# The edge stage of a graph kernel: 64-row products, a gathered layout with q left of x1, and copies moved between engines

## The reference

```python
h = silu(edge_scalars @ (Wfc1 / sqrt(16)));  w = h @ (Wfc2 / sqrt(64))
w0, w1, w2, w3 = w[:, :64], w[:, 64:128], w[:, 128:160], w[:, 160:192]
f0 = x0 @ Wl1_0 * a * inv8
f1 = einsum('num,uv->nvm', x1, Wl1_1) * a[..., None] * inv32
e0, e1 = f0[edge_src], f1[edge_src]
mid0 = w0 * e0 * sh0
mid1 = w3 * einsum('eum,em->eu', e1, sh1) / sqrt(3.0)
mid2 = w1[:, :, None] * e0[:, :, None] * sh1[:, None, :]
mid3 = w2[:, :, None] * e1 * sh0[:, :, None]
...
alpha = scal @ Wa * a * inv96;  out_s = scal @ Wl2_s * a * inv96
out_v = einsum('num,uv->nvm', vec, Wl2_v) * a[..., None] * inv96
x = layernorm(x + sc + alpha * concat([out_s, out_v]))
```

## Time and profile before

| what | value |
|---|---|
| time, median of 3 runs | 1123.99 us (1123.52 to 1131.0) |
| the profiled execution | 1131.23 us |
| its span, first to last instruction | 1129.4 us |
| mean granted clock of TensorE, of full speed | 0.981 |
| PE busy | 1029.3 us (91%) |
| PEld busy | 970.3 us (86%) |
| DVE busy | 975.0 us (86%) |
| ACT busy | 657.6 us (58%) |
| POOL busy | 752.1 us (67%) |

### The profile page before, as it was taken

The page is one execution under the profiler, slowest core; times in us unless marked ns, Lnnn a source line. Parts: engine busy times, 40 slices in busy tenths (PEclk is TensorE's granted clock), DMA queues, the critical chain, the costliest instruction groups (busy, mean ns, idle before and its releaser), DMA issues.

```text
span 1129.4 us, 33849 instructions
## 1 busy us (share of the span) xinstructions
PE 1029.3 (91%) x9020; PEld 970.3 (86%) x9020; DVE 975.0 (86%) x3758; ACT 657.6 (58%) x1865; POOL 752.1 (67%) x906
## 2 busy tenths in 40 slices
PE   4879999999999999999999869889988998898983
PEld 3869999999999999999999858777877887788883
DVE  3858888888888888888888849999999999999996
ACT  1324444444444444444444328888888888888877
POOL 6646666666666666666666247777777778778783
PEclk8989999999999999999999989999999999999997
DMA  5743343334334343434333268999999999999993
GB/s 161 156 134 109 103 112 103 109 103 112 109 105 110 98 115 103 112 102 110 106 108 111 68 167 217 253 242 246 257 254 241 247 254 252 244 251 249 261 249 106
DMA packets 170169, 184.95 MB, mean 164 GB/s; under 512 B 17831, under 2 KB 150247, under 8 KB 170152
## 3 DMA queue, kind: packets, MB, share of 16 engines
q1 hardware_dynamic: 151208, 152.15, 48.5%
q0 software_dynamic: 18944, 32.60, 13.9%
HBM read 119.73 MB, written 64.95 MB: 164 GB/s over the span
## 4 chain that ended last, share of the span: by engine, by line
PE 63%; DVE 13%; issue 9%; SPq 5%; POOL 3%; DMA 3%; ACT 3%; DVEq 0%; POOLq 0%; ACTq 0%
PE ps L646 15%; PE ps L659 10%; PE ps L636 7%; PE ps L710 5%; PE ps L654 4%; PE ps L634 4%; PE ps L625 4%; PE ps L619 4%; PE ps L656 3%; SPq L463 3%; DVE pre L1032 3%; PE ps L723 2%; DVE ra L1048 2%; PE ps L616 2%; DVE shift L1091 2%
## 5 line engine op out<-in xcount | busy, mean ns | idle before, releaser
L541 POOL DMA_INDIRECT gat<-table,src_now x392 | 374.1, 954 | 219.0 <-issue 115.7
L764 ACT ACTIVATE z<-ps 128x130 f32<-128x130 f32 x196 | 55.2, 282 | 291.7 <-PE ps L659 286.2
L578 POOL TENSOR_TENSOR xa<-xin 128x256 f32<-128x256 f32 x196 | 161.7, 846 | 94.9 <-DMA xin<-table 80.9
L646 PEld LDWEIGHTS ps<-h_sb,wt 128*128 128x128 f32 x1568 | 207.5, 193 | 11.6 <-issue 1.1
L646 PE MATMUL ps<-h_sb,wt 128*128 128x128 f32 x1568 | 208.0, 276 | 0.7 <-DVE mid L877 0.7
L805 ACT ACTIVATE fin<-res,shift,rstd 128x160 f32<-128x160 f32 x392 | 172.1, 511 | 53.8 <-DVE shift L1091 53.3
L710 PE MATMUL ps<-win,hot 64*128 64x162 f32 x2352 | 190.5, 308 | 4.0 <-ACT agg L796 3.9
L710 PEld LDWEIGHTS ps<-win,hot 64*128 64x128 f32 x2352 | 166.7, 187 | 22.6 <-issue 17.4
L597 POOL TENSOR_TENSOR res<-agg,pre 128x640 f32<-128x640 f32 x98 | 151.4, 1545 | 27.6 <-ACT agg L796 26.1
L659 PE MATMUL ps<-wy,mid 128*128 128x161 f32 x784 | 151.5, 316 | 0.0
L900 DVE SCALAR_TENSOR_TENSOR msg<-ps,sha,z 128x161 f32<-128x161 f32 x392 | 132.8, 381 | 4.9 <-ACT z L764 0.3
(11 more groups left out here) (102 smaller groups left out, 2046.2 us busy)
## 6 DMA issues: line engine op xcount, KB each, us to landing
win<-rows SPq DMA_DIRECT2D x392, 122.2 KB, 3.5
rows<-msg SPq DMA_DIRECT2D x98, 326.0 KB
xin<-table SPq DMA_DIRECT2D x98, 322.0 KB, 4.1
out<-fin SPq DMA_DIRECT2D x49, 640.0 KB, 5.3
gat<-table,src_now POOLq DMA_INDIRECT x392, 2.6
eas<-ea_t SPq DMA_DIRECT2D x5, 512.0 KB
wt<-weights SPq DMA_DIRECT2D x1, 929.5 KB, 4.7
shs<-sh_t SPq DMA_DIRECT2D x1, 752.0 KB
```

The source lines that it names most:

```text
L541: pool.indirect_dma_start(out=gat[:, n, 0:XW], out_offset=None, in_=table, in_offset=bass.IndirectOffsetOnAxis(ap=src_now[:, n:n + 1], axis=0)
L578: last = nc.gpsimd.tensor_tensor(xa[:, b0], xin[:, b, :, n:n + w], xin[:, b, :, 0:1].broadcast_to([P, GROUP, w]), ALU.mult)
L646: last = nc.tensor.matmul(w_ps[:, c, :], wt[:, w:w + P], h_sb[:, b1, :], start=True, stop=True)
```

## The change

All of it is in the edge stage, apart from the place of columns that the node stage reads.

- **w** is made by four products of 64 rows, one per tile and half of the columns, that use rows 0 to 63 and 64 to 127 of the array in turn and write into two banks, in place of four products of 128 rows. **e0** is made by two products of 64 rows in place of one of 128, and stands behind e1 now. The product for e1 is the same.
- **y** has two products of 97 columns and two of 161, before one of 130, one of 64 and two of 161.
- The nodes' rows are in three tables now, `table`, `turned` (x1, a, x0) and `spread` (x0, a, 32 zeros, x1). A pair's first tile is gathered from turned (161 columns), the second from spread (193), so that the x0 of both tiles lie side by side and PE can transpose them where they are: DVE's copy to `x0` goes. q lies left of x1 in both tiles.
- **mid** is one DVE instruction of 512 columns, before two of 256. ACT's copy of e is two instructions of 256 columns, before one of 384.
- The **label column** of msg is copied by ACT, before by DVE; DVE's msg waits for it by `label_ready`. DVE's **z** waits for ACT's copy (`zc_ready`), before for y itself.
- Before the loop, the row of heads goes to banks of w, PE waits there for `mid_ready`, DVE copies heads and the sum of wrong out of PSUM, and the fourth step's w waits for that.

```diff
-        e_ps = ps[:, 2, 0:3 * P].rearrange("p (c e) -> p c e", e=P)
-        w_ps = ps[:, 3, :].rearrange("p (c e) -> p c e", e=P)
-        y_ps = ps[:, 4, 0:2 * YW].rearrange("p (s w) -> p s w", s=2)
-        yb_ps = ps[:, 5, 0:2 * MUL1].rearrange("p (s w) -> p s w", s=2)
-        heads_ps = ps[:, 6, 0:T]
-        wrong_ps = ps[0:1, 7, 0:1]
+        e0_ps = ps[:, 2:4, 0:P]
+        e1_ps = ps[:, 2, P:3 * P]
+        w_ps = ps[:, 4:6, 0:2 * P]
+        y_ps = ps[:, 6:8, 0:YW]
+        heads_ps = ps[:, 4:6, 2 * P:2 * P + T // 2]
+        wrong_ps = ps[0:1, 4, 2 * P + T // 2:2 * P + T // 2 + 1]
...
                 pool.sem_inc(gather_go, 1)
-                for n in (2 * j, 2 * j + 1):
+                for s, of, first in ((0, turned, G_TURNED), (1, spread, G_SPREAD)):
+                    n = 2 * j + s
                     pool.indirect_dma_start(
-                        out=gat[:, n, 0:XW], out_offset=None, in_=table,
+                        out=gat[:, j, first:first + of.shape[1]], out_offset=None, in_=of,
...
-                    nc.tensor.transpose(t_ps[:, 0, :],
-                                        x0[:, b0].rearrange("p s w -> p (s w)"), ident[:])
+                    nc.tensor.transpose(t_ps[:, 0, :], gat[:, j, G_X0:G_X0 + P], ident[:])
                     for s in range(2):
                         last = nc.tensor.transpose(t_ps[:, 1 + s, :],
-                                                   gat[:, 2 * j + s, 1 + MUL0:GW], ident[:])
+                                                   gat[:, j, G_Q[s]:G_Q[s] + P], ident[:])
...
-                    nc.tensor.matmul(e_ps[:, 0, :], wt[:, W_E0:W_E0 + P], t_sb[:, b1, 0, :],
+                    nc.tensor.matmul(e1_ps, wt[:, W_E1:W_E1 + P],
+                                     t_sb[:, b1, 1:3, :].rearrange("p s e -> p (s e)"),
                                      start=True, stop=True)
-                    nc.tensor.matmul(e_ps[:, 1:3, :].rearrange("p s e -> p (s e)"),
-                                     wt[:, W_E1:W_E1 + P],
-                                     t_sb[:, b1, 1:3, :].rearrange("p s e -> p (s e)"),
-                                     start=True, stop=True).then_inc(e_ready, 1)
+                    for s in range(2):
+                        half = slice(s * MUL0, (s + 1) * MUL0)
+                        last = nc.tensor.matmul(e0_ps[:, s, :], wt[half, W_E0:W_E0 + P],
+                                                t_sb[half, b1, 0, :], start=True, stop=True)
+                    last.then_inc(e_ready, 1)
 
                     pe.wait_ge(h_out, done(i, j, 1))
                     if has(i, j, 2):
                         pe.wait_ge(mid_ready, done(i, j, 2))
-                    for c in range(4):
+                    if isinstance(i, int) and (i, j) == (0, 3):
+                        pe.wait_ge(heads_out, 2)
+                    for c in range(2):
                         w = W_W + c * P
-                        last = nc.tensor.matmul(w_ps[:, c, :], wt[:, w:w + P], h_sb[:, b1, :],
-                                                start=True, stop=True)
+                        for s in range(2):
+                            half = slice(s * FC_H, (s + 1) * FC_H)
+                            last = nc.tensor.matmul(w_ps[:, s, c * P:(c + 1) * P],
+                                                    wt[half, w:w + P], h_sb[half, b1, :],
+                                                    start=True, stop=True)
                     last.then_inc(w_ready, 1)
                 if alive(i, j, 2):
 
                     pe.wait_ge(mid_ready, done(i, j, 2))
                     if has(i, j, 3):
                         pe.wait_ge(msg_ready, done(i, j, 3))
-                    nc.tensor.matmul(y_ps[:, :, 0:1 + MUL0], mid[:, b2, 0, :],
-                                     wy[:, 0:W_YB - W_Y0], start=True, stop=True)
-                    nc.tensor.matmul(yb_ps.rearrange("p s w -> p (s w)"), mid[:, b2, 1, :],
-                                     wy[:, W_YB - W_Y0:W_Y1 - W_Y0], start=True, stop=True)
                     for s in range(2):
-                        last = nc.tensor.matmul(y_ps[:, s, 1 + MUL0:YW], mid[:, b2, 2 + s, :],
-                                                wy[:, W_Y1 - W_Y0:W_S0 - W_Y0],
+                        nc.tensor.matmul(y_ps[:, s, 0:W_Y1 - W_YA], mid[:, b2, s, 0:P],
+                                         wy[:, 0:W_Y1 - W_YA], start=True, stop=True)
+                        last = nc.tensor.matmul(y_ps[:, s, W_Y1 - W_YA:YW],
+                                                mid[:, b2, s, P:2 * P],
+                                                wy[:, W_Y1 - W_YA:W_S0 - W_YA],
                                                 start=True, stop=True)
                     last.then_inc(y_ready, 1)
...
+                pe.wait_ge(mid_ready, 2)
+                for n in range(2):
+                    last = nc.tensor.matmul(heads_ps[:, n, :], ones[0:1, :],
+                                            heads[:, n * (T // 2):(n + 1) * (T // 2)],
+                                            start=True, stop=True)
+                last.then_inc(heads_spread, 1)
...
-                    nc.scalar.activation(e_sb[:, b1].rearrange("p c e -> p (c e)"),
-                                         e_ps.rearrange("p c e -> p (c e)"),
-                                         ACT.Copy).then_inc(e_out, 1)
+                    nc.scalar.activation(e_sb[:, b1, :, P:2 * P],
+                                         e1_ps.rearrange("p (s e) -> p s e", s=2), ACT.Copy)
+                    nc.scalar.activation(e_sb[:, b1, :, 0:P], e0_ps, ACT.Copy).then_inc(e_out, 1)
+                if alive(i, j, 3):
+                    i3 = i if j == 3 else i - 1
+                    j3 = (j - 3) % PAIRS
+
+                    if has(i, j, 3 + PAIRS):
+                        act.wait_ge(messages_out[j3 // 2], 16 * (i3 + 0))
+                    else:
+                        act.wait_ge(dsts_ready, 1)
+                    nc.scalar.activation(msg[:, 2 * j3:2 * j3 + 2, LABEL],
+                                         dsts[:, bass.ds(i3 * BLOCK + 2 * j3, 2)],
+                                         ACT.Copy).then_inc(label_ready, 1)
                 if alive(i, j, 2):
...
-                    if has(i, j, 2):
-                        dve.wait_ge(t_ready, done(i, j, 2))
-                    nc.vector.tensor_copy(x0[:, b0], gat[:, n:n + 2, 1:1 + MUL0])
                     dve.wait_ge(qprod_ready, done(i, j))
-                    nc.vector.tensor_reduce(gat[:, n:n + 2, QX:GW], qprod[:], AX_X,
+                    nc.vector.tensor_reduce(of_pair(j, G_Q, MUL1), qprod[:], AX_X,
                                             ALU.add).then_inc(q_ready, 1)
...
-                    nc.vector.tensor_tensor(mid[:, b0, 0:2, :], w_ps[:, 0:2, :],
-                                            e_sb[:, b0, 0:1, :].broadcast_to([P, 2, P]),
-                                            ALU.mult)
-                    nc.vector.tensor_tensor(mid[:, b0, 2:4, :], w_ps[:, 2:4, :],
-                                            e_sb[:, b0, 1:3, :], ALU.mult
+                    nc.vector.tensor_tensor(mid[:, b0], w_ps, e_sb[:, b0], ALU.mult
                                             ).then_inc(mid_ready, 1)
                 if alive(i, j, 3):
 
-                    dve.wait_ge(y_ready, done(i, j, 3))
+                    dve.wait_ge(zc_ready, done(i, j, 3))
                     if has(i, j, 5):
                         dve.wait_ge(msg_ready, done(i, j, 5))
                     nc.vector.tensor_tensor(
                         z[:, b1, :, 1 + MUL0:].rearrange("p s (v m) -> p s v m", m=3),
-                        yb_ps.unsqueeze(3).broadcast_to([P, 2, MUL1, 3]),
+                        y_ps[:, :, 0:MUL1].unsqueeze(3).broadcast_to([P, 2, MUL1, 3]),
                         sha[:, j3, :, 1:4].unsqueeze(2).broadcast_to([P, 2, MUL1, 3]),
                         ALU.mult).then_inc(zb_ready, 1)
-                if alive(i, j, 3):
-
-                    if has(i, j, 3 + PAIRS):
-                        dve.wait_ge(messages_out[j3 // 2], 16 * (i3 + 0))
-                    nc.vector.tensor_copy(msg[:, 2 * j3:2 * j3 + 2, LABEL], dsts[:, at(i3, j3)]
-                                          ).then_inc(label_ready, 1)
-                if alive(i, j, 3):
+                    dve.wait_ge(label_ready, done(i, j, 3))
                     dve.wait_ge(zb_ready, done(i, j, 3))
                     dve.wait_ge(zc_ready, done(i, j, 3))
                     for s in range(2):
                         last = nc.vector.scalar_tensor_tensor(
-                            out=msg[:, 2 * j3 + s, 0:1 + D], in0=y_ps[:, s, 0:Y_C],
+                            out=msg[:, 2 * j3 + s, 0:1 + D], in0=y_ps[:, s, Y_A:Y_C],
                             scalar=sha[:, j3, s, 0:1], in1=z[:, b1, s, :],
                             op0=ALU.mult, op1=ALU.add)
                     last.then_inc(msg_ready, 1)
...
```

(9 more changed lines are left out.)

97 lines of the change are left out of this document (53 added, 44 removed).

## The result

The changed kernel takes 1368.62 us (median of 4 runs, 1367.36 to 1372.94) against 1123.76 us of the kernel before (4 runs, 1121.31 to 1131.0): a ratio of 1.2146, 95% interval 1.2101 to 1.219. It is slower by 245 us, and the forecast was 1366, with 1325 to 1440 as its range. The profiled run took 1372.94 us, with a span of 1371.1.

The account below looks back on a forecast made before the run. PE bounds the kernel before at 3.10 us per pair; the label on ACT closes a ring of waits of 4.40. 182 x 1.30 = 237 us plus 5 on the median of 1124 gives 1366 us, range 1325 to 1440.

Parts of the forecast that it names:

- Two halves for the price of one: PE's w and e0: two 64-row products cost one full product, so w takes 0.45 us in place of 0.89.
- The switch, 0.21 us: PE, between full and 64-row products: each change costs about 0.21 us, two per step.
- PE's own sum, 3.07: PE's work per pair after the change: 3.07 us against 3.10, saving 5 us over 182 pairs by itself.
- POOL, 2.92 and up to 3.5 for longer rows: POOL's gathers: 2.92 us per pair, at most 3.5 with spread's longer rows, both under the pace found.
- The label decides: ACT's label behind its e copies closes a ring of waits through DVE's msg and PE: 4.40 us per pair, not 3.10.
- from the reduction's end to the waiting transpose with a bare load: DVE's reduction to PE's next transpose: 0.15 us plus an unhidden load of 0.11, read at pair 4.
- the way through y: From msg through PE's y to the next transposes: 4.31 us per pair, a little less than 4.40 through DVE's reduction.
- Ahead of the loop and the last pairs: Pairs 4 to 13: 5 us added, between 0 and 12, with changed code ahead of the loop within that.
- The open ring: Rival: label is there when msg wants it; 1119 us, or 1091 without switch costs; 5 in 100 for both.
- The free switch: Rival: label's ring holds but changing between full and 64-row products costs nothing; 4.20 us per pair, 1329 us; 4 in 100.
- The falling clock: Rival: PE rests, its clock falls from 2.4 to 1.2 GHz; 5.8 us per pair, 1615 us; 6 in 100.
- What would show it: Trace signs: 4.3 to 4.5 us per pair, PE idle 1.1 ahead of y, msg waiting 1.4 for the label.

Follow-up runs that it names:

- e1: Not a run: a product PE makes in the edge stage, the same before and after the change; 0.43 us from start to start in full_rows.
- full_rows: Changed kernel with ACT's label copy at the head of its step and w and e0 as products over all 128 rows, zeros in unwanted weights: 1167.61 us, ratio 1.0349.
- label_first_3: Changed kernel with ACT's label copy at the head of its step, on a chip where the kernel before takes 1127.47 us: 1122.99 us, ratio 0.9953.
- e0_first: Changed kernel with ACT's label copy at the head of its step and e0's products ahead of e1, four switches per step, not two: 1234.59 us, ratio 1.0178.
- label_first: Changed kernel with ACT's label copy at the head of its step, where the kernel before takes 1212.98 us: 1207.3 us, ratio 0.9968.
- before_label_act: Kernel before with only the label moved to ACT, behind its copy of e, and msg waiting for it: 1306.1 us against 1212.98, ratio 1.0752.
- label_between: Changed kernel with ACT's label copy between the two e copies, not behind both: 1320.57 us, where the kernel before takes 1126.4.
- label_after_h: Changed kernel with ACT's label copy behind its h copy and ahead of both e copies: 1163.68 us, where the kernel before takes 1126.4.
- after_again: Changed kernel run again with no edit, on a chip where the kernel before takes 1126.4 us: 1369.77 us.

## Why the prediction was right

**What bounds the kernel before.** PE's row of work at 3.096 us per pair. full_rows and label_first_3 are also bound by it, at 3.318 and 3.044, and the total moves with it: 182 x 0.274 = 50 us, 1167.61 - 1122.99 = 45 between them.

**Two halves for the price of one.** Right. In label_first_3 w takes 0.54 and e0 0.33 from start to start, which is 0.45 and 0.22 with 0.1 of a switch on each, where full_rows has 0.90 and 0.44. In the changed kernel none of it shows in the time, since PE rests 1.21 us in each step.

**The switch, 0.21 us.** Right: 0.20 by full_rows against label_first_3, and 0.20 by e0_first against label_first, 3.44 to 3.04 for two more. It was read off two idle times of PEld in the node stage, which is another place with other shapes, and carried over. Where it is seen differs a little from what was said: the first border shows as 0.33 us idle of PEld ahead of e0 (0.2 predicted), but PE had the longer products of e1 to stream meanwhile; what PE loses is 0.10 there and 0.11 in e0's first load, which nothing hides.

**PE's own sum, 3.07.** Measured 3.044 in label_first_3. With the ring open, the 5 us saved became 182 x 0.052 = 9.5 in the pairs of the profiled run and 4.5 in the medians (1127.47 to 1122.99), whose single runs spread from 1115.53 to 1127.5.

**POOL, 2.92 and up to 3.5 for longer rows.** Nothing was lost there: POOL held 3.044 us per pair in label_first_3, at 329 us busy of 500. The ACT and DVE instructions that went or shrank gave nothing that could be seen, as said.

**The label decides.** Right in kind (label_first_3 takes the 245 us away, before_label_act brings a loss of 93 without the rest of the change), in place (label_between, label_after_h) and in size. The prediction's terms of unknown price were small and came out so: the label 0.24 with its way to DVE against 0.25, and the copies 0.54 against 0.52, though 0.39 long each. The one term that was too long is the last, from the reduction's end to the waiting transpose with a bare load, 0.26. Where the reduction releases PE, the product starts 0.05 to 0.06 behind its end (398.84 to 398.89), and the bare load makes its record 0.33 long in place of 0.27: 0.11 in all. The waiting transpose of pair 4 was a poor stand-in, because the granted clock was at half, 1.2 GHz, in that stretch, as the kernel before's windows show:

```profile
33.00:36.00 3.00, 2.69 (x11) 2.54 (x12) 2.84 (x13) 0.78 (x3) 2.10 (x3) 0.50 0.89 312
```

With 0.11 the way through the reduction is 4.25, and the way through y, which the prediction put second with 4.31, is the longer one by its own sum. It measured 4.29 to 4.35 where it ends last. So the prediction's 4.40 came from the wrong one of two nearly equal ways; the mean of 4.355 lies 0.045 below it, 182 x 0.045 = 8 us too many.

**Ahead of the loop and the last pairs.** 5 us were taken for pairs 4 to 13 with 0 to 12 as bounds; in the profiled run 10.0 were lost ahead of pair 13 (7.0 in after_again), and 2.7 us behind pair 195 weren't in the sum. These 8 us and the 8 too many per pair cancel. So part of the closeness of 1366 and 1368.62 is luck, some 8 us of it; each error alone would have left the time inside the range.

**The rivals.** The open ring is what label_first_3 is, 1122.99 us. The prediction had 1119 for it, and knew what it would take (a label 1.4 us earlier). The free switch fell to full_rows and e0_first. The falling clock did not come in the stage that counts: the granted clock was 1.00, though PE rested 28% of the time (361.43 of 500 busy).

**What would show it.** Nearly all of the signs came: a pair at 4.355 (4.3 to 4.5), PE idle for 1.21 us ahead of y (1.1), msg waiting 1.51 for the label in the step shown (1.4), the label right behind the second e copy, the node stage as before. PEld's idle time ahead of e0 is 0.33 (0.2), w's eight records take 0.54 with a switch in them (0.45 without), and an idle time of PE ahead of the transposes shows in one step of four only, as PEld's 0.19.

## What to carry to other kernels

When an instruction moves to another engine, don't ask how long it takes, ask what stands ahead of it in the new row and who there waits for whom: 0.2 us of label made a ring of 4.3 us out of pieces that nobody waited for before, and moving it past one 0.38 us copy was worth 49 us. A ring is read by following semaphores through one step until an engine comes back, and its length is the sum of start-to-start distances, which traces gave here within 0.1 us for kernels that had not run. Read each distance from rows at the clock that the ring will have, and add up every way round: here two were within 0.1 us. And before a step is costed by PE's streams alone, count the changes of row form: at 0.20 us each here, two of them took 0.40 of the 0.67 that the halves saved against full rows, and of the 0.45 against the kernel before.
